# Query and key parts of an attention layer: the order of six bf16 products, and the access pattern of the loads that stack them

## What is computed

```python
Q, K, V = (proj(Wq), proj(Wk), proj(Wv))            # 16 heads of 8
scores = jnp.einsum('bhqd,bhkd->bhqk', Q, K) / SCALE
idx = _rel_idx(s)
rel_k = pek[idx]
scores = scores + jnp.einsum('bhqd,qkd->bhqk', Q, rel_k) / SCALE
...
attn = jax.nn.softmax(scores, axis=-1)
```

## Time and profile before

| | before |
|---|---|
| runs, us | 971.23 median of 3 (966.93 to 976.51) |
| profiled execution | 967.66 us, its span 965.9 us |
| mean granted TensorE clock | 0.842 of full speed |
| TensorE busy (matmul) | 636.5 us, 66% |
| VectorE, ScalarE, GpSimd busy | 504.7, 297.2, 235.6 us |
| DMA | 73.27 MB; hardware queue 23.4% of 16 engines' time |

### The profile page before, as it was taken

One profiled execution on the slowest core, in us unless ns is written; L12 is line 12 of the kernel. 1 busy time (PEld: TensorE's weight loads), 2 busy tenths in 40 slices (PEclk: granted clock), 3 DMA queues, 4 the chain that ended last, 5 costly groups with the idle time before them and its releaser, 6 DMA issues.

```text
span 965.9 us, 29195 instructions
## 1 busy us (share of the span) xinstructions
PE 636.5 (66%) x12366; PEld 516.7 (53%) x12366; DVE 504.7 (52%) x1712; ACT 297.2 (31%) x473; POOL 235.6 (24%) x227
## 2 busy tenths in 40 slices
PE   4512998700733789888898879899972811689640
PEld 3501556500422678777787768788862800357430
DVE  7977222123721567565666557667766777512120
ACT  2390454300522232323232313232332264063210
POOL 2000738884533000000000000014110000346864
PEclk9999999955885599999898979999985555599985
DMA  4272213325355332323222323234342506112322
GB/s 122 59 218 80 53 17 43 34 24 142 132 160 173 92 62 70 59 69 60 69 44 74 52 70 56 65 72 97 75 110 46 175 1 178 24 35 31 45 25 22
DMA packets 99163, 73.27 MB, mean 76 GB/s; under 512 B 26569, under 2 KB 92258, under 8 KB 98914
## 3 DMA queue, kind: packets, MB, share of 16 engines
q1 hardware_dynamic: 85858, 57.01, 23.4%
q0 software_dynamic: 13184, 14.43, 9.2%
HBM read 44.34 MB, written 27.01 MB: 74 GB/s over the span
## 4 chain that ended last, share of the span: by engine, by line
PE 38%; DVE 15%; POOL 14%; issue 11%; ACT 9%; SPq 6%; DMA 5%; DVEq 0%; ACTq 0%; POOLq 0%
PE banks L1002 10%; ACT arena L778 8%; PE banks L1005 7%; POOL x_mid L554 5%; PE banks L1025 5%; POOL out_dram L554 5%; SPq L469 3%; DVE arena L1119 3%; PE banks L1066 2%; PE banks L849 2%; POOL arena L543 2%; PE banks L929 2%; PE banks L913 1%; DMA out_dram<-arena 1%; SPq L440 1%
## 5 line engine op out<-in xcount | busy, mean ns | idle before, releaser
L778 ACT ACTIVATE arena<-banks 128x1024 f32<-128x1024 f32 x96 | 98.3, 1024 | 263.4 <-PE banks L1025 263.4
L1002 PE MATMUL banks<-arena 128*128 128x32 bf16 x3072 | 126.8, 194 | 42.8 <-issue 16.1
L1002 PEld LDWEIGHTS banks<-arena 128*128 128x128 bf16 x3072 | 112.4, 101 | 68.1 <-ACT arena L778 38.7
L1366 DVE TRANSPOSE_TENSOR_REDUCE arena<-banks 128x32 f32<-128x1024 f32 x96 | 120.0, 1250 | 18.1 <-PE banks L1005 13.8
L1005 PE MATMUL banks<-arena 128*128 128x32 bf16 x3072 | 108.6, 178 | 8.6 <-issue 8.6
L1005 PEld LDWEIGHTS banks<-arena 128*128 128x128 bf16 x3072 | 93.6, 97 | 11.3 <-issue 11.3
L543 POOL DMA_INDIRECT arena<-table,arena x64 | 61.5, 961 | 126.2 <-DVE arena L1276 107.7
L607 POOL COPY arena<-arena 128x576 f32 (+1 forms) x8 | 5.3, 668 | 329.6 <-PE banks L1056 329.6
L1382 DVE TENSOR_REDUCE arena<-banks 32x8 f32<-32x64 f32 (+1 forms) x96 | 20.1, 209 | 107.9 <-PE banks L1017 107.8
L710 ACT ACTIVATE arena<-banks,arena 128x512 f32<-128x512 f32 x64 | 44.0, 687 | 85.2 <-PE banks L929 85.2
L1025 PE MATMUL banks<-arena 128*128 128x64 bf16 x1536 | 64.4, 198 | 0.7 <-issue 0.7
(11 more groups left out here) (182 smaller groups left out, 1021.4 us busy)
## 6 DMA issues: line engine op xcount, KB each, us to landing
query_parts<-arena SPq DMA_DIRECT2D x8, 768.0 KB, 6.4
arena<-query_parts SPq DMA_DIRECT2D x16, 384.0 KB
table<-arena SPq DMA_DIRECT2D x2, 2176.0 KB, 9.4
arena<-in_L_ffn_fc2s_dram SPq DMA_DIRECT2D x4, 1024.0 KB, 10.8
arena<-query_parts SPq DMA_DIRECT2D x16, 256.0 KB
key_parts<-arena SPq DMA_DIRECT2D x8, 384.0 KB, 7.0
arena<-key_parts SPq DMA_DIRECT2D x8, 384.0 KB
head_outputs<-arena SPq DMA_DIRECT2D x128, 18.0 KB
```

Source lines behind the costliest of these rows:

```text
L778: nc.scalar.activation(dst, psum[:, 2 * r:2 * r + 2, :].rearrange("p u (h n) -> p u h n", h=H), ACT.Exp, scale=HD ** -0.5).then_inc(s_prob, 1)
L1002: pe.matmul(sc[:, :, 2 * a:2 * a + 2], rel_k[:, y:y + P], q_st[:, r, :, q0 + 2 * a:q0 + 2 * a + 2], start=(a == 0), stop=False, skip_group ...
L1366: step(v.tensor_reduce(mp, psum[:, 2 * (s % 3):2 * (s % 3) + 2, :].rearrange("p u (h n) -> p (u h) n", n=32), AX.X, ALU.max, apply_transpo ...
```

## The change

```diff
-        Q_PART = (0, 0, 0, 1, 1, 2)
-        K_PART = (0, 1, 2, 0, 1, 0)
+        Q_PART = (0, 1, 2, 0, 1, 0)
+        K_PART = (2, 1, 0, 1, 0, 0)
         RUNS = ((0, 3), (3, 5), (5, 6))
...
                     lanes = slice((TERMS * c + a) * HD, (TERMS * c + b) * HD)
-                    q = qs[c, Q_PART[a], 0:HD, :, bass.ds(pr * PT, PT)]
-                    q = q.unsqueeze(0).to_broadcast([b - a, HD, H, PT])
-                    k = ks[0:b - a, :, :, bass.ds(pr * PT, PT)].rearrange("w d h n -> (w d) h n")
+                    q = qs[c, 0:b - a, :, :, bass.ds(pr * PT, PT)].rearrange("w d h n -> (w d) h n")
+                    k = ks[3 - (b - a):3, :, :, bass.ds(pr * PT, PT)].rearrange("w d h n -> (w d) h n")
                     yield q_st[lanes, r, :, :], q
                     if c == 0:
                         yield k_st[lanes, r, :, :], k
...
             if i % 2:
-                return k_part[:, i // 2 % 2, w, :]
+                return k_part[:, i // 2 % 2, 2 - w, :]
             return q_part[:, i // 2 % 2, 512 * w:512 * w + 512]
```

## The result

| | before | after |
|---|---|---|
| runs, us | 969.08 median of 4 (964.37 to 976.51) | 1015.88 median of 4 (1004.13 to 1018.19) |
| ratio to before, 95% interval | | 1.0451 (1.0345 to 1.0558) |
| profiled span, us | 965.9 | 1016.5 |
| mean granted TensorE clock | 0.842 | 0.772 |

The account below looks back on a forecast made before the run. It took the few DMA engines serving narrow loads to bound the projection stage. 22 us (first pair) plus 2.6 (pair 1), 24.6 off 967.66, gave 943.1, stated as 944; range 928 to 956.

Parts of the forecast that it names:

- The bound of the stage: Projection stage: the few DMA engines serving every narrow load hold it; their sum explains 44.4 of 49.4 us.
- The main term: First pair: last load lands, TensorE starts, at 290 instead of 311.92, -22 us; 17 off at the least.
- Rival (b): Projection stage: the compute chain holds it, TensorE starts at 297.5, 14.4 us off instead of 22, 951 us; chance 0.12.
- Pair 1: Pair 1: head stores go out well before, so the waits of ScalarE and TensorE behind them go; -2.6 us.
- Rival (d): Query loads: they stay narrow for another reason, 968 to 971 us; chance 0.05.
- Later pairs: 0 us: Loop after pair 1: TensorE never waits for a load in pairs 1 to 7, so nothing to gain, 0 us.
- rival (c): Pairs 1 to 6: code fetches queue behind the load burst, up to 9 us each, 29 us more, 997; chance 0.04.
- Rival (a): Loop: issue waits beside loads go, 10.3 us, perhaps 12, those at body heads may stay; 931 to 933 us; chance 0.15.

Follow-up runs that it names:

- e1: Changed kernel with a DRAM gap after each query part, so query loads again walk a first dimension of 3 or 2; 967.84 us, ratio 0.9935 to the kernel before.
- e7: Changed kernel with merged loads for the first pair only, loop loads on 3 and 2 engines as before; 946.62 us, ratio 0.9752 to the kernel before.
- e5: Changed kernel with the same loads spread over more destination partitions (scores not the reference's); 963.04 us, ratio 0.9896 to the kernel before.
- e6: Changed kernel with the loop's nine loads per pair issued one at a time, one per TensorE slot; 941.54 us, ratio 0.9667 to the kernel before.
- e8: Changed kernel without the loop's loads except those of pair 1 (scores not the reference's); 936.47 us, ratio 0.9615 to the kernel before.
- e2: Kernel with the old order of products, each repeat a load of its own, 15 loads a pair for 9; 1029.36 us, ratio 1.0614 to the kernel before.
- e9: Changed kernel with the loop's loads issued in three groups of three, after slots 0, 3 and 6; 976.65 us, ratio 1.0036 to the kernel before.

## Why the prediction was wrong

**The bound of the stage: right.** Narrow loads on three and two engines held the projection stage; e1 restores it with the access pattern alone, e7 gets the gain without the rest.

**The main term: right in kind, 5.4 us too large.** 22 us forecast, 16.6 measured, just below the 17 "at the least". The mis-sized number is 47 ns for 1 KB, read in one window of 1 us at the peak of a store. With loads and stores mixed on all engines the stage moved 264 GB/s at a share of 1.03 (the window 266 to 288), 16 x 1024 / 264 = 62 ns. With it, 528 KB on the busiest engine last 32.7 us from about 263, which gives 296; measured 295.31. The rate is taken from the changed stage itself, so this describes the miss and does not test it.

**Rival (b), the compute chain, is what happened in the stage**, and I had given it 0.12. It said that full DMA queues stretch four steps from 10.65 to 16 us, with step 12 at 281.8, the last load issued at 288.8 and TensorE's start at 297.5. These are steps 8 and 12 of ScalarE in the changed kernel, and the issue of the last load on SP:

```profile
266.83 0.59 ACT L725 CAST arena<-banks 128x512 bf16<-128x512 f32 x1 [0.16 <-DMA query_parts<-arena]
...
282.42 0.59 ACT L725 CAST arena<-banks 128x512 bf16<-128x512 f32 x1 [1.04 <-DMA query_parts<-arena]
```

```profile
289.10 0.68 SPq L446 DMA_DIRECT2D arena<-query_parts  x1
```

Four steps take 15.6 us, and the load lands 6.2 us after its issue. My 290 had kept the steps at 10.65 us, with step 12 at 276.4. ScalarE's waits for stores fell from 33.7 to 13.4 us, near the 10 forecast, but not away: with full engines the stores of earlier steps land late. e5 shows that the few partitions have a part in this: with spread destinations the stage moves 303 GB/s from 266 to 288, four steps take 13.5 us, and the first slot comes at 290.74.

**Pair 1: right in kind.** ScalarE waits for no head store any more between 300 and 700 us, but the 2.6 us drown in the new waits. **Rival (d)** falls: the loads did widen (e6 shows 12 engines).

**"Later pairs: 0 us": the step that failed.** I asked only whether TensorE waits for a load in those pairs, and it does not. I did not ask who else uses the engines that were idle. The rival (c) named the mechanism, fetches queued behind the burst, and its price of 29 us over before; I gave it 0.04 on two grounds, and both were weak. "TensorE ran without a pause at share 0.99" rested on a window of 1 us and eight matmuls, in which it may have needed no new code. The short waits beside narrow loads (the longest 3.6 us in the earlier trace rows, and not 3) were measured where 13 or 14 of the 16 engines stood free, and say nothing of a burst on all of them. And the 9 us of the burst were again reckoned at 47 ns a KB; it took 26 us, at 87 GB/s where the engines were fullest and at 57 at its end. No row of before shows a burst of loads without the narrow ones in front, but the window 375 to 376, at share 1.05 and only 200 GB/s, was there as a warning: the 16 engines were full and did three fifths of the work. Measured are 82 us of waits in pairs 1 to 6, 56 more than before, and 7.4 us in pair 0, which I had left out: 63 us more in all. The 54 us (6 x 9) that (c) added to the pairs are near the 56, but by luck: it took the burst for 9 us, and each pair to lose the whole of it, where the burst lasts 26 us and a pair loses about a third of it. Its 997 us came out too low since it set against this the full gain of 24.6 us, and left out pair 0 and the lower clock behind the waits.

**Rival (a)**, that issue waits beside narrow loads would go: the loads do cause those inside the pairs (e8 has none), but merging them makes more, not fewer. Its other half, that the waits at the head of a body stay whatever the loads do, is what e8 shows, at 11.8 us for two bodies.

**What is shown and what isn't.** Shown: the waits follow the number of engines that loads use (e1, e2), the time that the packets stay there (e5) and how many are queued (e9, e6), and go with the loads (e8). That the thing waited for is TensorE's code rests on the trace: the wait is for no semaphore, and each of the 109 waits ends 1.2 to 2.1 us after a packet of the instruction queue has landed. That q8 is TensorE's own queue is read from this agreement; the profile names no owner. The Trainium skill ("Runtime: NRT & Kernel Launch", Instruction fetch mechanics) says that the sequencer fetches its next page over a DMA queue of its own while it runs the current one, and the trace agrees with such a queue, whose packets are of 16 KB. No run here shows on which of the 16 engines a page comes, so that the fetch stands behind load packets on its engine, and is not held up somewhere else while loads are queued, is argued. It also stays open why the 16-engine burst into few partitions is slower than its loads one by one (184 and 151 GB/s in e6).

## What to carry to other kernels

A transfer confined to few DMA engines looks like waste, but in a long loop it may be what keeps the others free for instruction code; before widening loads, look for idle time of the busiest engine put down to issue, and ask what shares the DMA engines with it. Widen and pace together: issue each load when it fits, one per step of the computation, rather than all as soon as the buffer is free. And take the price of a packet from a window with the same mix and the same destination: GB/s over share, not GB/s alone, tells whether full engines are fast.

## What the runs showed of the hardware

- A burst of loads into 24, 16 and 8 partitions kept all 16 DMA engines busy (share 1.13) at 87 GB/s; over 96, 64 and 32 partitions it had 189 GB/s at 1.12. One load into 24 partitions at a time had 151 to 184 GB/s, on 12 engines (share 0.77 and 0.73 in e6).
- With nine, three and one load queued at a time TensorE lost 89.7, 47.0 and 22.2 us to issue; with none after those of pair 1, 19.1, of which 7.0 stand beside the loads of pair 1.
- All 109 issue waits of 2 us or more in twelve traces end 1.2 to 2.1 us after a 16 KB packet of the instruction queue has landed. Such a packet takes 0.9 to 2.9 us; in the changed kernel's waits of over 8 us it begins 5.2 to 7.2 us after TensorE has stopped.
- At the head of a loop body of this size, some 95 us of TensorE's time, it lost 5.8 to 6.0 us in two waits even with no load under way (3.61 and 2.38, 3.38 and 2.40 us).
- A DMA whose source walks a first dimension of 3 or 2 stayed on as many engines, whether that dimension repeats a row or not (e1: share 0.23 and 0.15 where the kernel before had 0.22 and 0.15, and 311.62 us for the first slot).
